# Between the attention loops of a fused attention and FFN kernel: maxima of the FFN's tiles in three parts, query's low halves and squares sooner, scores dealt anew among products

## What is computed

```python
def act_quant(x):
    scale = 127.0 / jnp.clip(jnp.max(jnp.abs(x), axis=-1, keepdims=True), 1e-05)
    return jnp.clip(jnp.round(x * scale), -128, 127) / scale
...
h = bit_linear(x, w1)            # 512 -> 2048, ternary weights, rows quantised to 8 bits
h = depthwise_conv1d(h.transpose(0, 2, 1), conv_w, conv_b)
h = jax.nn.silu(h.transpose(0, 2, 1))
return bit_linear(h, w2)         # 2048 -> 512
...
x = x + attention(_layernorm(x), ctx, ctx, Wq, bq, Wk, bk, Wv, bv, Wo, bo)
x = x + ffn(_layernorm(x), w1, conv_w, conv_b, w2)
```

## Time and profile before

| | before |
|---|---|
| median of three runs | 1520.56 us |
| the profiled execution's own time | 1520.43 us |
| its span, first to last instruction | 1518.6 us |
| TensorE busy | 96% of the span |
| VectorE busy | 84% |
| ScalarE busy | 78% |
| GpSimd busy | 68% |
| mean granted TensorE clock | 0.988 |

### The profile page before, as it was taken

One profiled execution on the slowest core, in us unless ns is written; L12 is line 12 of the kernel. 1 busy time (PEld: TensorE's weight loads), 2 busy tenths in 40 slices (PEclk: granted clock), 3 DMA queues, 4 the chain that ended last, 5 costly groups with the idle time before them and its releaser, 6 DMA issues. The chain is left out here.

```text
span 1518.6 us, 24856 instructions
## 1 busy us (share of the span) xinstructions
PE 1460.6 (96%) x9102; PEld 892.5 (59%) x9102; DVE 1278.0 (84%) x2002; ACT 1185.3 (78%) x2190; POOL 1028.7 (68%) x834
## 2 busy tenths in 40 slices
PE   9998988999999999999999999999999999999898
PEld 6474655657575665657575665657575655656343
DVE  5787796898979889898979898897979898887877
ACT  3567788979787888979687888979687888978763
POOL 4011567868675977968675977968675877968543
PEclk8999899999999999999999999999999999999999
DMA  8561002021310303030310303030210202020001
GB/s 258 148 193 42 29 8 71 8 80 32 76 43 12 94 8 99 8 93 19 75 44 18 88 8 99 8 100 14 73 43 23 84 8 71 8 71 1 31 1 56
DMA packets 80343, 85.21 MB, mean 56 GB/s; under 512 B 29983, under 2 KB 55839, under 8 KB 79709
## 3 DMA queue, kind: packets, MB, share of 16 engines
q1 hardware_dynamic: 80221, 83.62, 19.1%
HBM read 38.74 MB, written 19.42 MB: 38 GB/s over the span
## 5 line engine op out<-in xcount | busy, mean ns | idle before, releaser
L675 POOL TENSOR_TENSOR h<-h,gall 128x512 f32<-128x512 f32 x233 | 343.9, 1476 | 18.3
L660 POOL TENSOR_TENSOR h<-h,r 128x512 f32<-128x512 f32 x240 | 307.0, 1322 | 52.5 <-ACT r L1222 50.6
L673 POOL TENSOR_TENSOR gall<-gall,cw 128x512 f32<-128x512 f32 x233 | 255.3, 1096 | 112.6 <-DVE h L1751 112.6
L1751 DVE SCALAR_TENSOR_TENSOR h<-gall,cw,h 128x512 f32<-128x512 f32 x249 | 253.2, 1020 | 47.6 <-ACT h L1320 47.4
L885 PEld LDWEIGHTS ps<-va,pexp 128*128 128x128 f32 x2048 | 259.5, 192 | 29.0 <-issue 10.9
L1676 DVE SCALAR_TENSOR_TENSOR gall<-ps,bias,srow 128x512 f32<-128x512 f32 x256 | 191.1, 747 | 94.3 <-POOL h L675 57.9
L891 PE MATMUL ps<-xqT,w1T 128*128 128x512 f16 x1024 | 255.1, 379 | 6.6 <-DVE gall L1676 6.5
L885 PE MATMUL ps<-va,pexp 128*128 128x33 f32 x2048 | 257.7, 270 | 0.0
L1085 PE MATMUL ps<-w2T,hqb 128*128 128x512 fp8e4 x960 | 242.4, 380 | 0.0
L1320 ACT ACTIVATE h<-gall,cb,cw 128x512 f32<-128x512 f32 x249 | 216.3, 869 | 8.3
L1301 ACT ACTIVATE pexp<-ps 128x512 f32<-128x512 f32 x320 | 179.8, 589 | 54.5 <-PE ps L854 27.9
(11 more groups left out here) (226 smaller groups left out, 2336.8 us busy)
## 6 DMA issues: line engine op xcount, KB each, us to landing
qs<-hl SPq DMA_DIRECT2D x192, 128.0 KB, 2.4
xr<-in_x SPq DMA_DIRECT2D x16, 1024.0 KB, 5.4
out<-xr SPq DMA_DIRECT2D x64, 256.0 KB
h<-in_L_ffn_w SPq DMA_DIRECT2D x8, 1024.0 KB, 5.4
srow<-in_L_xattn_bo SPq DMA_DIRECT2D x15, 256.0 KB, 3.3
kst<-kh_scratch SPq DMA_DIRECT2D x32, 38.5 KB
xr<-in_ctx SPq DMA_DIRECT2D x1, 1024.0 KB
h<-in_L_xattn_Wk SPq DMA_DIRECT2D x1, 1024.0 KB, 8.2
```

The source lines that it names most:

```text
L660: gp.tensor_tensor(hc(c), hc(c), r2[:], ALU.mult).then_inc(u_ok, 1)
L673: gp.tensor_tensor(right, right, cw[:, c, 2:3].to_broadcast([P, TB]), ALU.mult).then_inc(c2m_ok, 1)
L675: gp.tensor_tensor(hc(c), hc(c), right, ALU.add).then_inc(c2p_ok, 1)
L1751: ve.scalar_tensor_tensor(out=hc(c), in0=g[:, c % 4, 1:TB + 1], scalar=cw[:, c, 1:2], in1=hc(c), op0=ALU.mult, op1=ALU.add).then_inc(c1_ok, 1)
```

## The change

The maxima over the hidden tiles are taken in three parts: tiles 0 to 3 inside the attention loop, ahead of the last tile's taps, tiles 4 to 11 after the low halves of the attention's output, tiles 12 to 15 after the first residual; there are two merges instead of one. VectorE's `q_low` come in pairs ahead of the third and of the fourth residual. ScalarE squares row tiles 0 and 1 ahead of the centring of tile 2, and gives the offset of tile 1 there. On TensorE, in the 13 slots with `late_results`, the first two pairs of scores come right behind `mm2(0)`, ahead of `spread_scales`; `mm2(1)` is cut into 8, 4 and 4 matmuls, `mm2(2)` into four times 4, `mm2(3)` into pairs that begin at n = 8. VectorE's `result(1)` moves behind the fourth maximum. `pm_ok` now counts 5 in a slot.

```diff
                 def turn_pm():
-                    pe.wait_ge(pm_ok, at(s, 3, 2 if s == NB else 0))
+                    pe.wait_ge(pm_ok, at(s, 5, 0))
...
                 if s == NB - 1:
                     mm2(1, range(4, CT))
+                elif late_results(s):
+                    mm2(0)
+                    query_scores(0, 0)
+                    query_scores(0, 1)
                 elif do_a and do_m:
                     mm2(0)
                     mm2(1)
...
-                if do_a and do_m and s != NB - 1:
-                    mm2(2, range(0, 8))
+                if late_results(s):
+                    mm2(1, range(0, 8))
...
-                    if do_q:
+                    if do_q and not (late_results(s) and n < 2):
                         query_scores(n // NG, n % NG)
...
-                    if do_a and do_m:
-                        if n < 4:
-                            mm2(2, range(8 + 2 * n, 10 + 2 * n))
-                        elif n < 13:
-                            mm2(3, MM2_LAST[n - 4])
+                    if late_results(s):
+                        if n in (2, 3):
+                            mm2(1, range(4 * n, 4 * n + 4))
+                        elif 4 <= n < 8:
+                            mm2(2, range(4 * n - 16, 4 * n - 12))
+                        elif 8 <= n < 15:
+                            mm2(3, range(2 * n - 16, 2 * n - 14))
+                        elif n == 15:
+                            mm2(3, range(14, 15))
+                            mm2(3, range(15, 16))
...
                     centre(1)
                     if s == NB - 1:
                         diagonals(2, 4)
+                    square(0)
+                    square(1)
+                    if late_results(s):
+                        offset(1)
                     centre(2)
                     if s == NB - 1:
                         diagonals(4, 5)
                     centre(3)
-                    if late_results(s):
-                        offset(1)
-                    for i in range(TT):
-                        square(i)
+                    square(2)
+                    square(3)
...
+                    if do_f and do_a and c == CT + 1:
+                        absmax(0, 2, pm)
                     if do_f and c >= 2 and not on_pe(s, c - 2):
                         taps(c - 2)
...
                 if do_f and do_a:
-                    absmax(0)
-                    if s == NB - 1:
-                        residual(0)
-                    absmax(1)
-                    if s == NB - 1:
-                        residual(1)
-                    merge()
+                    absmax(2, 6, r2)
+                    merge(r2, 2)
+                    residual(0)
+                    absmax(6, 8, r2)
+                    merge(r2, 4)
+                    residual(1)
...
                 if do_a:
-                    if s < NB - 1:
+                    if s == 0:
                         residual(0)
                         residual(1)
+                    if s > 0 and do_q:
+                        q_low(0)
+                        q_low(1)
+                    centred_max(0)
                     residual(2)
-                    centred_max(0)
+                    if s > 0 and do_q:
+                        q_low(2)
+                        q_low(3)
+                    centred_max(1)
                     residual(3)
-                    centred_max(1)
...
-                if s > 0 and do_q:
-                    q_low(0)
-                    q_low(1)
...
                     norm2()
-                if s > 0 and do_q:
-                    q_low(2)
-                    q_low(3)
...
                     result(0)
-                    result(1)
+                    if not late_results(s):
+                        result(1)
...
                 for n in range(8 if s == 0 else 0, TT * NG):
                     if do_q:
                         maximum(n // NG, n % NG)
+                    if late_results(s) and n == 3:
+                        result(1)
```

More of the change, by code:

```diff
@@ L419, in score_tiles @@
             return range(NS * c // n, NS * (c + 1) // n) if c < n else range(0)
-        MM2_LAST = [range(2 * n, 2 * n + 2) for n in range(7)] + [range(14, 15), range(15, 16)]
         LATE = (TT - 1) * P
@@ L1756, in taps, with absmax, merge @@
                                                 in1=hc(c), op0=ALU.mult, op1=ALU.add).then_inc(c2_ok, 1)
[L1758 to L1767, removed]
+                def absmax(a, b, o):
                     dve.wait_ge(si_ok, at(s, CT, 2 * b - CT))
+                    if a == 6 and do_a:
+                        dve.wait_ge(pm_ok, at(s, 5, 3 - 5))
                     ve.tensor_reduce(o[:], h[:, a:b].rearrange("p a t e -> p t a e"), AX.XY, ALU.max,
                                      apply_absolute_value=True).then_inc(pm_ok, 1)
-                def merge_last(o, n):
-                    dve.wait_ge(pm_ok, at(s, 3, n - 3))
+                def merge(o, n):
+                    dve.wait_ge(pm_ok, at(s, 5, n - 5))
                     ve.tensor_tensor(pm[:], pm[:], o[:], ALU.max).then_inc(pm_ok, 1)
@@ L1909, in slot @@
                     if s == NB and c == 16:
-                        absmax_last(0, 4, pm)
+                        absmax(0, 4, pm)
                         fix_absmax()
@@ L1935, in slot @@
                 if s == NB:
-                    absmax_last(4, 6, r2)
-                    merge_last(r2, 2)
+                    absmax(4, 6, r2)
+                    merge(r2, 2)
                     fix_scales()
-                    absmax_last(6, 8, pexp[:, 0, :])
-                    merge_last(pexp[:, 0, :], 4)
+                    absmax(6, 8, pexp[:, 0, :])
+                    merge(pexp[:, 0, :], 4)
                 if s == 0:
```

## The result

The changed kernel takes 1561.32 us (median of four runs, 1557.66 to 1563.64), against 1520.55 us before on the same chip: a ratio of 1.0274, 95% interval 1.0255 to 1.0293. It is slower by 2.7%.

The account below looks back on a forecast made before the run. TensorE, 96% busy, bounds the kernel, with VectorE nearly balanced between the loops. 1520.4 + 31.2 (13 slots at 2.4) + 2 (slots 1 and 15) + 10.2 (half clock) = 1563.8 us; range 1543 to 1577.

Parts of the forecast that it names:

- The second wait: TensorE at the third pair of scores waits 2.35 us for VectorE's first maximum, in each of 13 slots.
- The first wait: TensorE at `turn_pm` waits 1.05 us for VectorE's later third residual.
- everything behind the next slot's start moves along with it: Scores, dequantisations and first layer norm shift with TensorE's later start; no size of its own.
- The slot, 2.4 us: Each of slots 2 to 14 grows by 2.4 us, 31.2 us over 13 slots.
- The bare trip to GpSimd: Behind `norm2`, nothing covers VectorE's wait for GpSimd any more: 1.3 us added before the first maximum.
- The clock, six of 13 slots: TensorE falls to half clock behind six of 13 waits, 1.7 us each: 10.2 us.
- Slots 1 and 15: They have the three parts and the third residual's wait, without the moved scores: a us each, 2 us together.
- Squares that come sooner win nothing: ScalarE's sooner squares gain nothing: squares 2 and 3 hang on the fourth residual, `norm2` on VectorE's queue too.
- the others are there: Remaining signs: later third residual, VectorE idle over 1 us behind `norm2`, spells of 0.50 clock, slots of 86.8 us or more.
- the 642 that was to prove the forecast wrong: Sign against the forecast: maxima of tiles 4 to 11 starting clearly ahead of 642 in slot 6's terms.
- the one by which the loop gives half back: Attention loop: SiLUs 1.2 us sooner against TensorE start the chain sooner, a slot loses 1.2 us; 1538 us, chance 0.09.
- The two about the clock: TensorE's clock holds in all slots, 1553.6 us, chance 0.18; or falls in every slot, 1575.7 us, chance 0.14.

Follow-up runs that it names:

- d1: The change with ten products put back ahead of the third pair of scores, nothing else altered: 1536.2 us, ratio 1.0104.
- a1: The change with TensorE's order of products and scores and `result(1)` put back as before: 1543.6 us, ratio 1.0148.
- c3: The change with TensorE's order and `result(1)` put back, and the third residual ahead of the first low halves and centred maximum: 1526.8 us, ratio 1.0041.
- e1: The change with GpSimd waiting for the fourth maximum of the scores before it scales hidden tiles, in slots 2 to 14: 1571.2 us, ratio 1.0359.
- a2: The kernel before with only TensorE's new order of scores and products and the later `result(1)`: 1572.3 us, ratio 1.0347.
- c2: The kernel before with four of the eight products ahead of the first scores moved behind them, in slots 2 to 14: 1512.4 us, ratio 0.9955.
- d2: The kernel before with six products fewer ahead of the first pair of scores: 1518.4 us, ratio 0.9984.
- b1: The change with TensorE's order, `result(1)` and the low halves' places as before, keeping the maxima in parts and sooner squares: 1519.5 us, ratio 0.9996.
- a3: The change with the queries' low halves back in their old places and `residual(2)` ahead of the first centred maximum: 1576.5 us, ratio 1.0371.

## Why the prediction was right

The time came out at 1561.3 where 1563.8 was forecast, and for the forecast's reason; that it came so close owes something to luck with the clock. By its own steps:

- *The second wait, 2.35 us at the third pair of scores, released by the first maximum.* Right: 2.05 in the trace with modelled ends, in ten slots; 1.53 in the three with masks. `d1` shows that it is the number of products ahead of it that makes it.
- *The first wait, 1.05 us at `turn_pm`.* Right in its cause and its size, wrong in its place. The maxima of tiles 4 to 11 start at 642.5 in slot 6's terms, as summed, and the third residual ends 1.4 us later than before against the loop's first product, where 1.1 were forecast. But TensorE stands at `turn_pm` in five slots only, 5.5 us in all, because it has already stood 0.85 us ahead of the query projection, 8.0 us in all. The text had said that everything behind the next slot's start moves along with it; that step failed: VectorE's tap took 1.83 us instead of 0.79 beside GpSimd. The two together make 13.5 us, near the 13 x 1.05 that were put down, since both are TensorE's waiting for the same third residual. Without the deal all of it stands at `turn_pm`, 1.6 us a slot (`a1`).
- *The slot, 2.4 us.* The quiet ones are 86.9 against 84.4, 2.5 us: 1.3 up to `turn_pm` and 1.3 from there to the next slot's first product (24.35 instead of 23.1; 24.5 was forecast).
- *The bare trip to GpSimd, 1.3 us.* Present, 1.13 idle. Alone, without the deal, it costs about 3.6 us in twelve slots (`c3`), since TensorE is not waiting for all of it.
- *The clock, six of 13 slots, 10.2 us.* Six it was in the profiled execution, 1.7 us each, and that it was exactly six is luck. The forecast took the middle between one wait that brought the half rate and one that did not. `e1` has waits of the same 2.05 us in the same ten slots and three spells. The other executions of the change have granted clocks of 0.980 to 0.984, and the one with 0.984 took 1557.7 us. The row of 1.66 us in slot 15 on which the forecast leaned was an exception: the same wait stands in the profiles of `a2`, `c2` and `d2` and no half rate follows it. Dummies in the wait give back 6.7 us by the medians and 9.4 by the profiles. The Trainium skill's rule (TensorE: Matmul & The Clock Gate, "Why this matters for your kernels"), that only longer gaps bring the half rate back, would have had none; the trace shows it behind six of the ten waits of 2.05.
- *Slots 1 and 15, a us each.* Slot 15's out-projection waits 3.07 us instead of 1.66, as the first part of the maxima finds no hole there. Slot 1 costs nothing: from its `turn_pm` to the next are 90.6 us, 90.7 before.
- *Squares that come sooner win nothing.* They were not tried alone; with the maxima in parts they came to nothing (`b1`).

Of the signs that were named, the wait at `turn_pm` is missing in most slots, and the wait of over 2 us at the third pair is 1.53 in the three with masks; the others are there. The maxima of tiles 4 to 11 would seem to start at 641.5, ahead of the 642 that was to prove the forecast wrong, if they were counted from `turn_o`; but `turn_o` itself had moved, and from the loop's first product it is 642.5.

The rivals: the one by which the loop gives half back was wrong in its mechanism. The SiLUs stand 1.1 us sooner against `turn_o`, but only because `turn_o` is 1.0 later; against the loop's first product they are where they were. The two about the clock bound what came, none and all of the slots. What neither the forecast nor the rivals had is that the low halves' new place is needed by the deal: put back, the change takes 1576 us.

## What to carry to other kernels

Where two engines meet at a rendezvous and both are nearly full, count the work that each has left ahead of it: products that were a cover for VectorE's chain turned into a stall when moved behind it, and of the places tried the best was four products from the old one, not twenty. A change of several parts can hold a part that pays only for another, so take each out alone, and look at all semaphores a moved instruction waits for. An engine with slack (GpSimd) that starts sooner can shift waits between the others; a wait that is new need not be a loss, if what comes behind it would have waited anyway. To see that, count times in both kernels from an instruction that has not moved.

## What the runs showed of the hardware

How often a wait of TensorE went over into half clock for 3.4 us (sometimes for twice that), at its end or within about a us behind it: at `turn_pm` none of 29 waits of 0.7 to 2.0 us (the change, `a1`, `e1`); at the third pair of scores none of six of 1.53 us, and of ten of 2.05 us six in the change and three in `e1`; of 13 of about 2.8 us 11 in `a2` and 11 in `a3`; at slot 15's out-projection one of four of 1.66 us, and all nine of 3.07 us; in slot 16, over all profiles here, nine of 13 of about 3.5 us. So the length of a wait alone does not decide. A spell on an engine that sets the end cost 1.7 us.

VectorE's tap on one tile took between 0.73 and 1.84 us in the change (mean 1.02 us before, 1.06 after). The 37 taps beside which GpSimd was idle took at most 0.77 us; each of the 84 that took over 1.2 us had GpSimd at work for more than half of its time.

The kernel before itself reads 1516 to 1525 us over all its runs, and the longer times go with the lower granted clocks: 0.992 with 1516.7 us, 0.983 with 1524.7. A difference of a few us between two single executions may be the clock's alone.
